# A selective-scan kernel: the first sequence's first step size made in two halves of 512 columns, and two loads of ScalarE's function table moved

## The reference

```python
uc = jax.nn.silu(uc)                       # after a convolution with 4 taps
dbl = uc @ xproj
dt, Bm, Cm = jnp.split(dbl, [DT_RANK, DT_RANK + N], axis=-1)
delta = jax.nn.softplus(dt @ dt_w + dt_b)  # the step size
A = -jnp.exp(Alog)
def step(h, inp):
    u_t, d_t, B_t, C_t = inp
    dA = jnp.exp(d_t[..., None] * A)
    h = dA * h + (d_t * u_t)[..., None] * B_t[:, None, :]
    y_t = jnp.einsum('bdn,bn->bd', h, C_t)
    return (h, y_t)
```

## Time and profile before

| what | value |
|---|---|
| runs | 1471.96, 1472.04 and 1476.65 us, median 1472.04 us |
| the profiled execution | 1476.72 us, of which the profile's span is 1474.9 us |
| mean granted TensorE clock | 0.897 of full speed |
| busy in the span | PE 1184.5 us, DVE 1149.8 us, POOL 884.9 us, ACT 771.7 us |

### The profile page before, as it was taken

The page is one execution under the profiler, slowest core; times in us unless marked ns, Lnnn a source line. Parts: engine busy times, 40 slices in busy tenths (PEclk is TensorE's granted clock), DMA queues, the critical chain, the costliest instruction groups (busy, mean ns, idle before and its releaser), DMA issues. The chain is left out here.

```text
span 1474.9 us, 14736 instructions
## 1 busy us (share of the span) xinstructions
PE 1184.5 (80%) x4924; PEld 659.2 (45%) x4924; DVE 1149.8 (78%) x1051; ACT 771.7 (52%) x1029; POOL 884.9 (60%) x394
## 2 busy tenths in 40 slices
PE   5999986797639897549986475484598999999998
PEld 3788832232103232113332121131146788787887
DVE  4344459999999999999999999999878654545445
ACT  4444466667645776555775555465256533343330
POOL 4530027999999999999999999999910000000000
PEclk9999998899959898769898678687799999999999
DMA  5344235442463234255123437313015030303012
GB/s 200 107 155 136 95 97 201 157 159 75 162 235 134 99 139 155 101 205 199 72 86 146 154 118 291 142 58 114 13 47 200 24 120 1 143 0 128 0 38 76
DMA packets 46016, 176.34 MB, mean 120 GB/s; under 512 B 5873, under 2 KB 10481, under 8 KB 33538
## 3 DMA queue, kind: packets, MB, share of 16 engines
q1 hardware_dynamic: 45954, 175.57, 32.8%
HBM read 142.78 MB, written 32.77 MB: 119 GB/s over the span
## 5 line engine op out<-in xcount | busy, mean ns | idle before, releaser
L1268 POOL TENSOR_TENSOR scan_dbu<-scan_rep,scan_bc 128x1024 f32<-128x1024 f32 x254 | 592.7, 2361 | 39.6 <-ACT scan_rep L1166 28.7
L1355 DVE TENSOR_TENSOR_SCAN scan_hs<-scan_hs,scan_dbu 128x1024 f32<-128x1024 f32 x191 | 436.7, 2286 | 11.6 <-ACT scan_hs L1193 10.1
L1193 ACT ACTIVATE scan_hs<-scan_rep,scan_neg_a 128x1024 f32<-128x1024 f32 x252 | 280.8, 1118 | 306.1 <-DVE scan_hc L1369 278.7
L1077 PE MATMUL scan_ysum<-scan_hc,scan_sel 128*32 128x512 f32 x1008 | 171.3, 812 | 206.5 <-DVE scan_hc L1369 190.3
L1369 DVE TENSOR_TENSOR scan_hc<-scan_hs,scan_bc 128x1024 f32<-128x1024 f32 x191 | 233.7, 1223 | 6.1
L1077 PEld LDWEIGHTS scan_ysum<-scan_hc,scan_sel 128*32 128x32 f32 x1008 | 35.5, 131 | 320.1 <-issue 269.5
L1274 POOL TENSOR_TENSOR scan_hc<-scan_hc,scan_bc 128x1024 f32<-128x1024 f32 x65 | 153.1, 2356 | 7.6 <-DVE scan_hc L1355 7.4
L1355 DVE TENSOR_TENSOR_SCAN scan_hc<-scan_hs,scan_dbu 128x1024 f32<-128x1024 f32 x65 | 148.1, 2279 | 0.8 <-POOL scan_dbu L1268 0.7
L938 PE MATMUL scan_banks<-late_xin,scan_inwf 128*128 128x512 f32 x256 | 115.2, 604 | 0.0
L32 PE MATMUL ffn_sl<-ffn_tanh_s,xm_s 128*128 128x512 f32 x384 | 107.3, 415 | 2.3 <-DVE ffn_tanh_s L2153 2.3
L1955 PE MATMUL ffn_oy<-ffn_y,ffn_et 128*128 128x256 f32 x448 | 102.0, 379 | 0.8 <-DVE ffn_y L2173 0.8
(11 more groups left out here) (274 smaller groups left out, 1820.4 us busy)
## 6 DMA issues: line engine op xcount, KB each, us to landing
scan_rep<-dd_rows SPq DMA_DIRECT2D x60, 1024.0 KB, 5.7
scan_bc<-bc_rows SPq DMA_DIRECT2D x32, 512.0 KB, 6.0
ffn_wt<-in_ew SPq DMA_DIRECT2D x16, 1024.0 KB, 7.8
dd_rows<-scan_dd SPq DMA_DIRECT2D x15, 1024.0 KB, 3.8
scan_bc<-gate_rows SPq DMA_DIRECT2D x24, 256.0 KB, 4.8
scan_inwf<-fold SPq DMA_DIRECT2D x12, 512.0 KB, 3.8
cond<-scan_bc SPq DMA_DIRECT2D x16, 256.0 KB, 3.1
y_all<-scan_yo SPq DMA_DIRECT2D x6, 512.0 KB, 3.1
```

The costliest lines, as they stand in the source:

```text
L1077: mm = nc.tensor.matmul(ysum[i * D32:(i + 1) * D32, h, :], sel[:], hc[:, (s0 + i) % HCR, h * CT:(h + 1) * CT], start=False, stop=last, til ...
L1193: nc.scalar.activation(hs[:, s % HSR, :], rep[:, e % REPS, 0, :], ACT.Exp, scale=scale).then_inc(da_done, 1)
L1268: nc.gpsimd.tensor_tensor(dbu[:, s % DBR, :], rep[:, e % REPS, 1, :], bc[:, j, 0, :], ALU.mult).then_inc(dbu_done, 1)
L1355: nc.vector.tensor_tensor_scan(states, hs[:, s % HSR, :], dbu[:, s % DBR, :], 0.0, ALU.mult, ALU.add).then_inc(scan_done, 1)
```

## The change

In the first period the step size is now made and used in halves. ScalarE runs |x|, exp and ln for half 0 and then for half 1 (first_step), VectorE adds and multiplies half 0 and then half 1 (first_du), and TensorE spreads each half as it comes: step, product, step, product for replica 0, and the rest as before. TensorE's skip product no longer waits for `soft`. Two table loads stand elsewhere: the one for SiLU comes after the first block's copies, not ahead of them, and the one for exp and ln comes ahead of the copies of the rows, not behind them. The exponential of A's logarithm and its sign come ahead of the step size. The counts that later waits use are adapted (soft_at, and one more count on du_done).

```diff
--- before.py
+++ after.py
@@ -765,8 +765,12 @@
             else:
                 freed(eng, *(("u", k, dc, h) for dc in dcs for h in range(HALVES)))
 
+        def soft_at(w):
+
+            return (HALVES + 2) * w + (2 * (HALVES - 1) if w else 0)
+
         def step_add(engine, eng, w):
-            eng.wait_ge(soft, (HALVES + 2) * (w + 1))
+            eng.wait_ge(soft, soft_at(w + 1))
             freed(eng, *(("t", *divmod(w, DC), h) for h in range(HALVES)))
             engine.tensor_tensor(dd[:, 0, :], dd[:, 0, :], dd[:, 1, :], ALU.add).then_inc(delta_done, 1)
 
@@ -784,6 +788,12 @@
             wait_delta(eng, w)
             wait_uc(eng, k, [dc])
             engine.tensor_tensor(dd[:, 1, :], dd[:, 0, :], uc[k % 2][:, dc, :], ALU.mult).then_inc(du_done, 1)
+
+        def first_du(dve, h):
+            freed(dve, ("t", 0, 0, h))
+            wait_uc(dve, 0, [0])
+            part = slice(h * CT, (h + 1) * CT)
+            nc.vector.tensor_tensor(dd[:, 1, part], dd[:, 0, part], uc[0][:, 0, part], ALU.mult).then_inc(du_done, 1)
 
         def wait_du(eng, e):
 
@@ -822,7 +832,7 @@
                 kinds = slice(0, 1 if w == 0 else 2)
                 wait_delta(sp, w)
                 if w > 0:
-                    sp.wait_ge(du_done, w + 1)
+                    sp.wait_ge(du_done, w + HALVES)
                 sp.dma_start(dd_rows[w % 2][:, kinds], dd[:, kinds]).then_inc(dd_out, 16)
 
             def load_rep(w, i):
@@ -981,27 +991,28 @@
                 else:
                     eng.wait_ge(hc_done, by_dve(s + 1))
 
-            def spread_step(i):
+            def spread_step(i, halves=range(HALVES)):
 
                 if i >= HSR:
                     wait_states(pe, i - HSR)
-                wait_delta(pe, 0)
-                for h in range(HALVES):
+                for h in halves:
+                    freed(pe, ("t", 0, 0, h))
                     mm = nc.tensor.matmul(hs[:, i % HSR, h * CT:(h + 1) * CT], spread[:, i * P:(i + 1) * P],
                                           dd[:, 0, h * CT:(h + 1) * CT], start=True, stop=True)
-                mm.then_inc(spread_done, 1)
-
-            def spread_du(i):
-
-                pe.wait_ge(du_done, 1)
-                for h in range(HALVES):
+                if HALVES - 1 in halves:
+                    mm.then_inc(spread_done, 1)
+
+            def spread_du(i, halves=range(HALVES)):
+
+                for h in halves:
+                    pe.wait_ge(du_done, h + 1)
                     out, done = claim(("r", i, h))
                     nc.tensor.matmul(out, spread[:, i * P:(i + 1) * P], dd[:, 1, h * CT:(h + 1) * CT], start=True, stop=True
                                      ).then_inc(done, 1)
 
             def step_total(k, dc, h):
                 out, done = claim(("a", k, dc, h))
-                pe.wait_ge(soft, (HALVES + 2) * (DC * k + dc + 1))
+                pe.wait_ge(soft, soft_at(DC * k + dc + 1))
                 freed(pe, *(("t", k, dc, i) for i in range(HALVES)))
                 for i in range(2):
                     mm = nc.tensor.matmul(out, ident[:], dd[:, i, h * CT:(h + 1) * CT], start=(i == 0), stop=(i == 1))
@@ -1093,9 +1104,11 @@
                     first_x_proj()
             pe.wait_ge(consts_in, 3 * 16)
             pe.wait_ge(diag_done, 2 * DC)
-            pe.wait_ge(soft, HALVES + 1)
             skip(0, 0)
-            for kind, i in FIRST_SPREADS:
+            for h in range(HALVES):
+                spread_step(0, [h])
+                spread_du(0, [h])
+            for kind, i in FIRST_SPREADS[2:]:
                 (spread_step, spread_du)[kind](i)
             for k in range(GROUPS):
                 for p in range(DC):
@@ -1146,16 +1159,23 @@
                 for h in range(HALVES):
                     x, free = ready(act, "t", k, dc, h)
                     nc.scalar.activation(dd[:, 0, h * CT:(h + 1) * CT], x, ACT.Abs).then_inc(soft, 1)
-                    if w == 0:
-                        continue
                     nc.scalar.activation(dd[:, 1, h * CT:(h + 1) * CT], x, ACT.Relu).then_inc(free, 1)
 
+            def first_step(h):
+                x, _ = ready(act, "t", 0, 0, h)
+                own = dd[:, 0, h * CT:(h + 1) * CT]
+                nc.scalar.activation(own, x, ACT.Abs).then_inc(soft, 1)
+                act.wait_ge(soft, 3 * h + 1)
+                nc.scalar.activation(own, own, ACT.Exp, scale=-1.0).then_inc(soft, 1)
+                act.wait_ge(soft, 3 * h + 2)
+                nc.scalar.activation(own, own, ACT.Ln, bias=1.0).then_inc(soft, 1)
+
             def step_exp(w):
-                act.wait_ge(soft, (HALVES + 2) * w + HALVES)
+                act.wait_ge(soft, soft_at(w) + HALVES)
                 nc.scalar.activation(dd[:, 0, :], dd[:, 0, :], ACT.Exp, scale=-1.0).then_inc(soft, 1)
 
             def step_ln(w):
-                act.wait_ge(soft, (HALVES + 2) * w + HALVES + 1)
+                act.wait_ge(soft, soft_at(w) + HALVES + 1)
                 nc.scalar.activation(dd[:, 0, :], dd[:, 0, :], ACT.Ln, bias=1.0).then_inc(soft, 1)
 
             def replica(i):
@@ -1204,19 +1224,19 @@
                 nc.scalar.activation(yo[:, cc, :], x, ACT.Copy).then_inc(free, 1)
 
             act.wait_ge(vecs, 6 * 16)
-            nc.scalar.preload_act_table_set("silu_and_others")
             for dc in range(DC):
                 for h in range(HALVES):
                     first_conv(dc, h)
-                if dc > 0:
+                if dc == 0:
+                    nc.scalar.preload_act_table_set("silu_and_others")
+                else:
                     first_silu(dc - 1)
             first_silu(DC - 1)
+            nc.scalar.preload_act_table_set("natural_log_exp_and_others")
             copy_rows(0)
-            nc.scalar.preload_act_table_set("natural_log_exp_and_others")
-            step_in(0, 0)
-            step_exp(0)
-            step_ln(0)
             nc.scalar.activation(neg_a[:], neg_a[:], ACT.Exp).then_inc(neg_done, 1)
+            for h in range(HALVES):
+                first_step(h)
             act.wait_ge(neg_done, 2)
             for kind, i in FIRST_SPREADS:
                 (decay, replica)[kind](i)
@@ -1378,14 +1398,14 @@
                     wait(dve, conv0, (TAPS - 1) * i + t)
                     nc.vector.scalar_tensor_tensor(own, u0[:, dc, lo * CT + t:hi * CT + t], taps[:, dc, t:t + 1], own,
                                                    ALU.mult, ALU.add).then_inc(conv0, 1)
-            dve.wait_ge(soft, HALVES + 2)
+            dve.wait_ge(neg_done, 1)
+            nc.vector.tensor_scalar(neg_a[:], neg_a[:], -1.0, None, ALU.mult).then_inc(neg_done, 1)
             for h in range(HALVES):
+                dve.wait_ge(soft, 3 * (h + 1))
                 x, free = ready(dve, "t", 0, 0, h)
                 own = dd[:, 0, h * CT:(h + 1) * CT]
                 nc.vector.scalar_tensor_tensor(own, x, 0.0, own, ALU.max, ALU.add).then_inc(free, 1)
-            step_du(nc.vector, dve, 0)
-            dve.wait_ge(neg_done, 1)
-            nc.vector.tensor_scalar(neg_a[:], neg_a[:], -1.0, None, ALU.mult).then_inc(neg_done, 1)
+                first_du(dve, h)
             for w in range(PERIODS):
                 k, p = divmod(w, DC)
                 for r in range(UPP):
```

## The result

The changed kernel takes 1473.45 us in the median of 20 runs (1468.24 to 1475.57), the kernel before 1476.96 us in the median of 20 (1471.96 to 1480.91). The ratio is 0.9977 (95% interval 0.9967 to 0.9986): 3.4 us less, between 2.1 and 4.9, against a forecast of 3.4. That the two are the same to the digit is partly chance: the interval is wide, and the start moved by 3.98 us, not by 3.4. The profiled execution of the changed kernel took 1473.87 us, its span is 1472.1 us.

What follows compares the result with a forecast made beforehand. VectorE bounds the Mamba stage; only its first input could move, from 222.12 to 218.7 us, when the rows land (218.67 + 0.05). That -3.4 us from 1472.04 gave 1468.6 us, range 1466.0 to 1473.3.

Steps and rivals of the forecast that it cites:

- the second row's 5.2 us: DMA time of the second of rows B and C, first quarter, taken as before the change; landing at 218.67.
- The SiLU load: ScalarE's table load of 1.28 us, moved behind the first block's copies: all that follows moves by -0.43 us.
- The exp and ln load beside the wait for the x projection: ScalarE's 1.28 us table load, hidden in the wait for the last x projection; copy 0 starts only 0.13 late.
- The rival of the longer loads: Each ScalarE table load costs 1.38 us more in its new place: gain only 0.8 us, 1471.2; chance 0.04.
- The halves: Step size in halves over ScalarE, VectorE, TensorE: exp and ln 0.63 us each; arithmetic allows first input at 217.98, 4.1 earlier.
- The rows bind: At VectorE's first input, DMA of rows B and C ends last, 218.67: input at 218.7, -3.4 us; chance 0.50.
- the rival of the sooner rows: Both rows take 3.5 us, there by 217.0, so the arithmetic sets the start: gain 4.1 to 4.3, 1467.9; chance 0.16.
- The lower clock: Rival: TensorE still falls to the lower clock, half spreads take 1.72 us each: gain 2.6, 1469.4; chance 0.08.
- A transfer takes the place: Rival: something behind needs the step size's replicas, which move only 1.3 us: gain 1.3, 1470.7; chance 0.08.
- Rows held up: Slower rival: the step size's write delays the rows' DMA; at 9.0 us for the second row, 1472.5; chance 0.06.
- The stage's length: Sign to check: first scan to the last of the Mamba stage as far apart as before, within 0.5 us.
- the case given 0.65: Whole kernel's time changes by less than 0.3%; faster by more was given 0.28, slower by more 0.07.

Runs made afterwards that it cites:

- halves_only: The changed kernel with both table loads back where they were: distance from the stage's first matmul to VectorE's first input 31.60 us, ratio 0.9977 against the kernel before.
- skip_free: The kernel before with only TensorE's wait ahead of the skip product taken out: distance 35.01 us, ratio 1.0009 against the kernel before.
- skip_free_busy: The kernel before without the wait ahead of the skip product, and with three extra matmuls keeping TensorE busy: distance 33.31 us, ratio 0.9984.
- b_row_alone: The changed kernel with VectorE's first input waiting for the B row alone, not the C row: distance 30.29 us, ratio 0.9976 against the kernel before.
- skip_waits: The changed kernel with TensorE's wait ahead of the skip product put back: distance 32.82 us, ratio 1.0003 against the kernel before.
- loads_only: The kernel before with only the two table loads moved: distance 33.50 us, ratio 1.0001 against the kernel before.
- rows_last: The changed kernel with the rows of the other three quarters loaded ahead of the first quarter's: distance 38.94 us, ratio 1.0048 against the kernel before.
- rows_late: The changed kernel with the 512 KB output-weight load issued ahead of the rows' first reload: distance 33.29 us, ratio 1.0006 against the kernel before.

## Why the prediction was right in the change and missed in the level

The time of 1473.45 us lies 0.15 us above the range, whose upper end was 1473.3. The step that failed is the base: "against 1472.04 I forecast 1472.04 - 3.4", and "the upper end is 1468.6 + 4.7". The 1472.04 was the median of three runs, two of which happened to be among the fastest; of the 20 runs of the kernel before that there are now, three lie below 1473 us, and the median is 1476.96, close to the profiled execution of 1476.72. From 1476.96 the forecast gain would have given 1473.6. The upper end added the three runs' whole difference to a full gain of 3.4, so nothing was left for the spread beyond those three: 20 runs reach 1480.91. What moves, and in what order, was forecast rightly; one term of the sum was too large, the second row's 5.2 us. Step by step, as distances from the stage's first matmul:

| step | forecast | measured |
|---|---|---|
| taps of blocks 1 to 3 start | 7.15 | 7.19 |
| copy 0 of the rows starts | 21.62 | 21.71 |
| ln of half 1 ends | 27.30 | 27.40 |
| last spread visible | 29.98 | 30.16 |
| second row landed | 30.82 | 30.2 |
| first input | 30.85 | 30.29 |

- *The SiLU load*: 0.43 forecast, 0.41 measured in two kernels.
- *The exp and ln load beside the wait for the x projection*: as forecast. No drain of 1.38 us lies behind a load in either place: the copy starts 0.01 us behind it. The rival of the longer loads is out, and the Trainium skill's 2.66 us for a switch ("ScalarE: Activation LUTs", "What ACT_TABLE_LOAD costs") does not hold here, its 1283 ns for the load itself does.
- *The halves*: exp and ln of 512 columns took 0.63 us each, the figure taken from tanh.
- *The rows bind*: half right. The second row took 4.5 us, not the 5.2 of before, was requested 0.33 sooner (not 0.43), and landed together with the last spread. The start moved by 3.98 us, between the forecast (3.4) and the rival of the sooner rows (4.1), nearer to the rival. The 5.2 was one draw of a time that varies: with the same requests the second row took 4.5 to 4.7 in the changed kernel, halves_only, skip_free, skip_free_busy and b_row_alone, and 5.2 to 5.6 in the kernel before, skip_waits and loads_only. With 5.6 in the changed kernel it would land at the distance 31.3 and the gain would be 2.9, an estimate from these times. So that rows and arithmetic end together holds for this one execution.
- *The lower clock*: did not come, as forecast. But the forecast counted the skip product's earlier start as if it were a detail. skip_free and skip_waits show, by one trace each, that it is one half of a pair: starting it early without the halves loses 0.74 us against the kernel before, and taking it away from the changed kernel loses 2.5 of the 3.98.
- *A transfer takes the place*: it did not. The first reader of the replicas that travel through DRAM, the decay of unit 4 (line below), starts 231.70 - 216.90 = 14.80 us behind the first input; before it was 236.92 - 222.12 = 14.80. It moved whole. rows_last alone could not show this, since there the replicas' requests came later as well (227.62, in the changed kernel 218.26).
- *Rows held up*: the mechanism exists. In rows_late a request of the rows took 7.2 us with other transfers around it. In the changed kernel it did not happen, though the write of the step size was issued at 214.81, with the second row still moving.
- *The stage's length*: forecast as unchanged within 0.5 us, measured 1.13 longer (843.06 against 841.93). That sign was set too tight: over the ten profiled executions the length lies between 840.59 and 846.10, and it does not follow the changes.
- *Chances*: the change in time stayed within 0.3% (0.23%), the case given 0.65.

```profile
231.70 1.15 ACT L1213 ACTIVATE scan_hs<-scan_rep,scan_neg_a 128x1024 f32<-128x1024 f32 x1
```

One thing is not settled: skip_waits has a distance 1.45 us below the kernel before, but its ratio is 1.0003, with an interval that begins at 0.9994, or -0.9 us. The other ratios agree with their distances within their intervals. Its profiled execution took 1474.91 us and is one of five between 1474.4 and 1474.9; the other six took 1476.2 to 1477.1, and none of them was profiled. They may have paid more at the start or elsewhere; the cause stays open.

## What to carry to other kernels

Ahead of a stage that one engine bounds for 800 us, its late start goes through to the end (10.2 us as 9.7 in rows_last, 3.0 as 2.6 in rows_late, within what the stage itself varies), and a chain of three engines can be shortened there by passing on halves, where the fixed costs of splitting are small beside the idle time: from the first |x| to the end of the last ln ScalarE took 3.73 us instead of 3.27, while VectorE had idled 8.40 us. Count the second condition of the wait as well: here the transfer was done within 0.1 us of the arithmetic, and its time varied by 1.1 us between executions. And a matmul placed early is only a gain if TensorE has something to do until it is needed; an idle gap ahead of a chain of matmuls can cost more than the early placing gains, as in skip_free.

## What the runs showed of the hardware

- The lower clock came after short idling: with 1.24 us of idling ahead of it, a product that takes 1.98 us took 3.54. At this place it also came after 1.87 (loads_only), 2.39 (before) and 2.89 us (skip_free), and not after 1.06 (halves_only) or less. The length of the gap alone does not tell: ahead of the x projection TensorE idled 1.6 to 1.8 us in each of the ten profiled executions, and the granted clock stayed at 1.00 there. The Trainium skill ("TensorE: Matmul & The Clock Gate", "Part 1: The HAM clock gate") says that the clock is set by how busy TensorE has been of late; the trace agrees, and with three matmuls in the idle time of 2.89 us the full clock stayed.
- Stages that no edit touches vary between executions by more than the change is worth. From the first input to the last product with the gate it was 840.59 us in one profiled execution and 846.10 in another, with VectorE's loop unchanged; its waits for ScalarE's decays came to 8.2 us in the first and 13.2 in the second (rows below, halves_only and loads_only). The 20 runs of the kernel before lie between 1471.96 and 1480.91 us, so three runs could not show a level.

```profile
DVE scan_hs L1374 <- ACT scan_hs L1213: 8.2, 18, 1.4
```

```profile
DVE scan_hs L1356 <- ACT scan_hs L1193: 13.2, 18, 2.2
```
